# Three small PSUM copies on ScalarE, moved in front of one pair of exponentials

## The reference, cut to what matters

```python
# x: (2, 512, 512), context: (2, 1024, 512), 16 heads of 32 dimensions
q = rms_norm(linear(layernorm(x), q_w, q_b), norm_q_w)
k, k_img = rms_norm(linear(ctx, ...))            # image part: 257 keys, text part: 767 keys
out = attention(q, k, v) + attention(q, k_img, v_img)
x = x + linear(out, o_w, o_b)
# feed-forward: a chain on the last token of each of the two sequences
x_norm = layer_norm(layernorm(x), in_gamma, in_beta)
thought = x_norm[:, -1, :] @ agg_w + agg_b
for _ in range(4):
    t = layer_norm(thought, pn_gamma, pn_beta)
    t = gelu(t @ d1_w + d1_b)
    thought = thought + (t @ d2_w + d2_b)
broadcast = (thought @ bc_w + bc_b)[:, None, :]
gate = sigmoid(x1 @ gate_w + gate_b)             # x1: layernorm(x), all tokens
x = x + layer_norm(x1 + gate * broadcast, out_gamma, out_beta)
```

## Time and profile before

| | |
|---|---|
| median of 3 runs | 519.63 us (519.6 to 520.52) |
| the profiled execution's own time | 518.58 us |
| its span, first to last instruction | 516.8 us |
| PE / PEld busy | 494.6 us (96%) / 319.4 us (62%) |
| DVE / ACT / POOL busy | 351.0 (68%) / 302.7 (59%) / 254.5 us (49%) |
| mean granted TensorE clock | 0.992 of full speed |

### The profile page before, as it was taken

The page is one execution under the profiler, slowest core; times in us unless marked ns, Lnnn a source line. Parts: engine busy times, 40 slices in busy tenths (PEclk is TensorE's granted clock), DMA queues, the critical chain, the costliest instruction groups (busy, mean ns, idle before and its releaser), DMA issues.

```text
span 516.8 us, 9804 instructions
## 1 busy us (share of the span) xinstructions
PE 494.6 (96%) x3734; PEld 319.4 (62%) x3734; DVE 351.0 (68%) x781; ACT 302.7 (59%) x548; POOL 254.5 (49%) x157
## 2 busy tenths in 40 slices
PE   8999999999899999999999999999999999999990
PEld 7988878777666666656665555454544455545440
DVE  5379846877787778749784876565656485427677
ACT  4883466543276667736873466666663566667553
POOL 1330033320067779848886544352525374739563
PEclk9999999999999999999999999999999999999996
DMA  8997577497997799986999793525252473000011
GB/s 286 390 301 268 198 163 230 166 213 278 275 261 186 189 309 205 250 229 181 238 275 235 182 267 112 127 68 132 64 137 64 139 202 123 6 22 22 26 37 61
DMA packets 61439, 91.92 MB, mean 178 GB/s; under 512 B 4496, under 2 KB 29344, under 8 KB 60816
## 3 DMA queue, kind: packets, MB, share of 16 engines
q1 hardware_dynamic: 56992, 74.68, 53.9%
q0 software_dynamic: 3280, 14.51, 8.8%
q10 hardware_dynamic: 1120, 2.10, 1.3%
HBM read 71.87 MB, written 19.66 MB: 177 GB/s over the span
## 4 chain that ended last, share of the span: by engine, by line
PE 78%; DVE 13%; ACT 3%; DMA 3%; issue 2%; DVEq 0%; SPq 0%; ACTq 0%
PE psum L876 13%; PE psum L984 13%; PE psum L1003 13%; PE psum L967 12%; PE psum L1051 6%; PE psum L1008 5%; PE psum L1160 3%; PE psum L1096 3%; PE psum L1116 3%; DMA qscr<-hl 2%; PE psum L898 2%; DVE hl L1481 1%; DVE negt L1494 1%; DVE hl L1480 1%; PE psum L881 1%
## 5 line engine op out<-in xcount | busy, mean ns | idle before, releaser
L1266 ACT ACTIVATE prob<-psum 128x512 f32<-128x512 f32 x256 | 138.9, 595 | 97.1 <-PE psum L984 78.3
L1494 DVE TENSOR_REDUCE negt<-psum 128x1 f32<-128x512 f32 (+1 forms) x256 | 133.1, 546 | 17.3 <-PE psum L967 17.1
L1770 POOL TENSOR_TENSOR added<-added,prob 128x1024 f32<-128x1024 f32 x48 | 114.7, 2389 | 11.8 <-ACT prob L1266 7.0
L984 PEld LDWEIGHTS psum<-qst,kst 112*128 112x128 f32 x512 | 77.2, 188 | 36.0 <-ACT prob L1266 17.1
L984 PE MATMUL psum<-qst,kst 112*128 112x256 f32 x512 | 97.8, 307 | 1.3 <-ACT prob L1266 1.0
L1767 POOL TENSOR_TENSOR added<-prob 128x1024 f32<-128x1024 f32 x16 | 38.0, 2374 | 112.9 <-ACT prob L1266 112.9
L967 PE MATMUL psum<-kst,qst 96*128 96x512 f32 x256 | 85.3, 429 | 4.8 <-DVE negt L1494 3.6
L1003 PE MATMUL psum<-prob,vring 128*32 128x256 f32 x1152 | 83.5, 387 | 0.3 <-ACT prob L1266 0.3
L1492 DVE TENSOR_REDUCE negt<-psum 128x1 f32<-128x257 f32 x128 | 53.0, 414 | 45.2 <-PE psum L967 45.1
L967 PEld LDWEIGHTS psum<-kst,qst 96*128 96x128 f32 x256 | 42.8, 188 | 35.1 <-issue 15.7
L1003 PEld LDWEIGHTS psum<-prob,vring 128*32 128x32 f32 x1152 | 27.6, 108 | 20.9 <-ACT prob L1266 0.8
(11 more groups left out here) (189 smaller groups left out, 711.7 us busy)
## 6 DMA issues: line engine op xcount, KB each, us to landing
kst<-kscr SPq DMA_DIRECT2D x96, 256.0 KB, 6.3
vring<-vscr SPq DMA_DIRECT2D x16, 576.0 KB, 7.2
kscr<-hl SPq DMA_DIRECT2D x16, 512.0 KB, 3.2
d<-d POOLq DMA_DIRECT2D x8, 1024.0 KB, 9.3
qst<-qscr SPq DMA_DIRECT2D x48, 128.0 KB, 4.2
vscr<-vbuf SPq DMA_DIRECT2D x18, 256.0 KB, 3.3
qscr<-hl SPq DMA_DIRECT2D x8, 512.0 KB, 3.0
in_c<-ctxT SPq DMA_DIRECT2D x2, 1024.0 KB, 13.1
```

The source lines that it names most:

```text
L984: mm = pe.matmul(score2[:, j * QH:(j + 1) * QH], kst[0:96 + 4 * HPG, slot, jj, k0:k0 + P], qst[0:96 + 4 * HPG, slot, jj, :], start=True, s ...
L1266: act.activation(prob[:, r % NP, part], score2[:, part], ACT.Exp).then_inc(exp2_done, 1)
L1494: dve.tensor_reduce(negt[:, u % 2, qt, half, HPG + j:HPG + j + 1], psum[:, tile_bank[n], k0:512], AX.X, ALU.max, negate=True)\
L1770: pool.tensor_tensor(added[:, :], added[:, :], prob[:, r % NP, :], ALU.add).then_inc(added_done, 1)
```

## The change

`ch_gather` is put `behind` in step 73, right after `ch_agg`, in place of `at` in step 74.

```diff
@@ -226,7 +226,7 @@
         s = 8 * (9 + k)
         if k == 0:
             behind(s + 1, 'ch_agg', 0)
-            at(s + 2, 'ch_gather')
+            behind(s + 1, 'ch_gather')
             at(s + 2, 'ch_stat', 2)
         behind(s + 2, 'ch_ln', 2 + k)
         at(s + 3, 'ch_copy', 2 + k)
```

## The result

The changed kernel takes 516.83 us (median of 20 runs, 515.89 to 519.95) against 519.62 us of the kernel before (20 runs, 518.17 to 524.0). The ratio is 0.9945 with a 95% interval of 0.9929 to 0.996: 2.1 to 3.7 us faster. The forecast was 518.1 us with a range from 517.1 to 519.6.

A forecast was written before the change was run, and what follows sets the result against it. The late gather held VectorE and so TensorE, busy 96% of the span. VectorE's chain gains 1.54 us, TensorE's 1.63; the smaller, taken as 1.5, off the 519.63 us median gives 518.1 us, range 517.1 to 519.6.

The forecast's parts named there:

- What bounds it: Around the gather: VectorE waits 1.56 us for it, then TensorE lacks a free bank for S1(87) and idles 0.81 us.
- When the gather runs: On ScalarE: copies start at 305.44, 0.13 us behind the product's end, take 0.72 us and end at 306.16.
- The estimate of 1.2 us for three copies: ScalarE's gather by the skill page's budget: copies end near 306.7, gain about 1.1 us; the trace's 0.72 us disagrees.
- What waits behind it: Exponentials of step 74 start at 306.18 in place of 306.12; S2(75) has no slack for this delay.
- d: Delay of ScalarE's exponentials of step 74 by the copies put in front of them: 0.06 us.
- The rival of the late product: ScalarE sees the product 0.26 us late, so the gather starts at 305.70: gain 1.32, time 518.3 us; chance 25%.
- the unexplained 0.26 us: From S2's start to ScalarE's exponentials: 0.88 us at the gather against 0.62 us behind the other thin product.
- The sum: ch_d1 needs VectorE's chain (1.54 us earlier) and TensorE's (1.63 us), so it moves by the smaller, taken as 1.5.
- TensorE's own bound: S2(76), without waits in S1(87), ends at 309.47 in place of 311.10: 1.63 us earlier.
- TensorE is on the path up to 418 us and each engine is driven by it: Behind ch_d1, no load or other wait holds TensorE, so the 1.5 us gain lasts to the end.
- The range: 517.1 us from best sum 1.63 and run spread 0.9; 519.6 us from the late-product case with the same spread.
- The median against the profile: Median of the runs shown is 1.05 us above the profiled execution, so 518.1 us was forecast in place of 517.1.

The follow-up runs named there:

- e2: Changed kernel with three more copies of the same size behind the gather's three, in front of the exponentials of step 74: 517.72 us, ratio 0.996.
- n4: Kernel before, unedited, third of four single runs: 522.38 us, clock 0.987.
- e3: Kernel before with three unused matmuls in TensorE's 0.8 us wait before the second tile of S1(87), gather still late: 518.88 us, ratio 0.9979.
- e6: Kernel before with three unused matmuls in TensorE's two short waits at 290 to 293 us, wait before S1(87) left open: 520.32 us, ratio 0.9989.
- n0: Kernel before, run again unchanged under another name, 12 runs: 520.42 us, ratio 1.0004.
- e1: Kernel before with VectorE's statistics put behind the reductions of S1(86), gather still late: 521.06 us, ratio 1.0008.
- e4: Changed kernel with nine more copies behind the gather's three, in front of the exponentials of step 74: 523.15 us, ratio 1.0057.
- n1: Kernel before, run once more unchanged as a set of 12 runs: 519.45 us, ratio 0.9995.
- n3: Kernel before, unedited, second of four single runs: 520.36 us, clock 0.987.

## Why the prediction was right in direction and wrong in size

- *What bounds it:* right. The late gather held VectorE, VectorE a bank, and TensorE stood still; all three waits are gone, and the way from `ch_d1` on is no longer than it was. From `ch_d1` to the end both profiles have 202.8 us.
- *When the gather runs:* right. It starts 0.07 us behind the product's end (0.13 forecast) and takes 0.72 us. The estimate of 1.2 us for three copies, by the Trainium skill, page "ScalarE: Activation LUTs", section "Rules for kernel authors", does not hold here.
- *What waits behind it:* d was 0.06 by the sum and is 0.00. The rival of the late product did not come about: the copies start 0.14 us behind `S2(74)`. That d is nothing is in part luck, since the copies end where the exponentials used to start. So this profile cannot show whether the exponentials, without copies in front of them, would still come the unexplained 0.26 us late; what that 0.26 us was stays open. And `S2(75)` does have slack for d: by e2, a quarter of a microsecond.
- *The sum, "it moves by the smaller: 1.54 us":* mis-sized by 0.13 us. VectorE's next instruction starts 0.33 us behind a reduction's start (307.77 to 308.10), not at its reported end 0.42 behind it, so that the statistics moved by 1.65 relative to `S2(74)` (2.74 to 1.09 us). TensorE's own bound came out as forecast: `S2(76)` ends 4.23 us behind the start of `S2(74)` in place of 5.86, which is 1.63, and 0.04 us more are won from there to `ch_d1`. That makes the 1.67 measured.
- *The step that failed* is the sentence that ends the sum, that behind `ch_d1` "TensorE is on the path up to 418 us and each engine is driven by it", with nothing else to lose or win. The sum has no term for TensorE's clock: it puts it at nothing, without a reason. (In the profiled execution the clock is indeed full from 300 to 460 us.) In nearly half of the executions of the kernel before it is not full throughout. Where the low stretch follows the idle 0.81 us, as in n4, it lasts 6.8 us and costs 2.7 us; and with that wait filled (e3) no run is low. The change takes the low clock away together with the wait. In means over all sets, the spans of before are 518.01 us, and 516.92 us where the clock is full, so the low clock costs it 1.09 us; the changed kernel has 515.43 and 515.20 us, a cost of 0.23 us. The gain is therefore 1.72 us at full clock and 0.86 us by the clock, 2.58 us of the mean span. The medians that were compared, 2.79 us apart, lie somewhat further from each other, because that of before falls between its runs with a full and with a low clock.
- *The range* ended at the best sum of the full clock plus the spread of three runs. No case on the fast side had the clock in it. The Trainium skill, page "TensorE: Matmul & The Clock Gate", section "A second HAM failure mode: psum-queue depth-cycling", tells of a kernel in which TensorE idles briefly between its groups of matmuls, often enough that the clock goes back and forth between its two levels. By that, a removed wait can be worth more than its length; the experiments with the filled wait (0 of 12 runs low) and with the lengthened ones (11 of 12, 10 of 10) agree.
- *The median against the profile:* I set the forecast 1.05 us above the profiled execution as if that were a constant. It was a first sign of the clock: the profiled execution was one of the runs at full clock, whose median time is 518.8 us over the 51 such runs beside the others, and the median of all lies between these and the low ones (520.2 us and more).

What stays open is how the low clocks of the kernel before are shared out between the places. Only one of its seven profiles shows the long stretch behind `S1(87)` (a second is that of e6), one has a low stretch at 268 us, and two have one at 294 us, while only 4 of 43 runs of the changed kernel are low at all, although it is the same up to 307 us. Chance can make both. That the wait before `S1(87)` is the main place rests on the lists of runs of e3 and e6, not on the profiles.

## What to carry to other kernels

A short wait of a TensorE that is otherwise busy can cost more than its length, and not in every execution: look at the granted clock of each run beside its span, and take several, before a profile's clock is taken as given. If the spans of a kernel fall in two groups that go with the clock, fill the suspected wait with matmuls of no use: if the low group goes while the way keeps its length, the low clock hangs on that wait. And where an engine's queue has an idle stretch in front of an instruction that waits for something else, work that is already ready belongs in that stretch, with its own wait in front of the other.

## What the runs showed of the hardware that I had not expected

- A wait of 0.8 us, of a TensorE that was otherwise busy, was followed by a granted clock of 0.5 (1.2 GHz) for 6.8 us in two profiles (n4 and e6); in the six other profiles of the kernel before it was not. 16 of 35, 16 of 33 and 13 of 27 runs of that kernel have a low mean clock, with those from the places at 268 and 294 us among them. With a wait of 1.46 us it was 11 of 12, with 1.99 us 10 of 10, with three matmuls in the 0.8 us 0 of 12.
- The length of the wait does not decide alone: in the profile of the changed kernel TensorE waits 1.65 us for queries at 265.6 us, and its clock stays full from 262 to 275 us. In n0 a wait of 1.92 us at the same place is followed by 3.4 us at 1.2 GHz.
- The fall can come well behind the wait: in n4 TensorE ran at full clock again for 1.3 us (310.04 to about 311.36), in e1 for some 2.5 us. In e4 it came at the end of the wait itself, at 308.8 us.
- At 1.2 GHz the eight matmuls of L1003 take 1.08 us in place of 0.64. The low clock of 6.8 us cost 2.7 us of time in n4, that of 3.4 us some 1.5 us in n1 and n3.
- A load of queries that takes longer than usual holds TensorE for 1.6 to 1.9 us near 267 us in some executions of either kernel.
